# Batch 0's router one unit earlier, its weight transposes ahead of z(61), the last P's lo half shared by GpSimd and VectorE

## The chip, the cores and the metric

One core of a Trainium2 chip runs the whole program. The metric is the device time of one execution in microseconds; the profile of one execution stands beside it. The engines are TensorE (PE, its weight loads PEld), VectorE (DVE), ScalarE (ACT), GpSimd (POOL) and SyncE (SP, which here only issues DMAs). Each engine takes its instructions in program order and waits on semaphores.

## What is computed

An adaLN transformer block in float32 on x of 4 batches x 512 positions x 256 columns:

```
h = layernorm(x) * (1 + ca) + sa
k, q, v = W_K h, W_Q h, W_V h                    # 16 heads of 128
attn = softmax(causal(k.q) / sqrt(128)); z = attn v
x = x + ga * (W_O z)
h = layernorm(x) * (1 + cb) + sb
logits = h @ router_w + router_b - cost          # 8 experts
gate, top = softmax over the two largest of softmax(logits)
out = sum over the two of gate * expert(h @ down_w + down_b)
x = x + gb * ((out + 0.1 shared) @ up_w + up_b + gelu(h) @ core_w + core_b)
```

Every product is made of three TensorE passes on a hi and a lo half of both operands (`mm3`, L680 to L682): hi is the operand rounded to fp32r, lo is the rest, subtracted by VectorE or GpSimd.

## The kernel before, in words

**Order.** One list of events, made by `attention_plan` and `ffn_plan`, is walked by every engine, and each takes from it what is its own, in that order. So the place of an event in the list is its place in up to five queues. Attention runs over 64 units u (4 groups of 4 heads x 4 batches x 4 heads, `unit`), one turn i of the loop per unit, some 10.2 us each. A turn holds the scores S(i+2), q(i+3), `ri` (reciprocal of the sums), k(i+3), `norm` (scaling of P), `wo` (W_O product of an earlier pair), `ty` (VectorE transposes of P in 32x32 blocks, L1076 to L1079), v, `pt`(i+1), z(i) and `tr`(i+2). `fill[i]` is a list of groups of events: the first goes behind S, the next ones behind q, wo, v and z, the rest to the end of the turn. `pre[i]` goes ahead of z(i), `post[i]` to the end.

**P.** `norm` and `ty` leave a transposed P in `gab`; `tr` sends it by four DMAs from SP (L462) to `ptl`, where its blocks come together; `pt` makes its hi half on ScalarE (two casts of 128x640, L650) and its lo half on GpSimd (two subtractions of 128x640, L547, each after its cast). z(u) waits for both (`s_pl`).

**Banks.** The events of `MISC` (q, k, v, z, wo, h, h2, r, wt, dn and others) share three PSUM banks in turn: event m waits until event m-3 is emptied (`me`, counted by VectorE). VectorE empties q, k, v and z by a subtraction (L1049), behind ScalarE's cast (L639).

**Layer norm of the FFN's input** for batch b: `st` steps 0 to 3 (L1004, L1009, L1013) on VectorE, a pow on GpSimd (L490) behind step 3, two pieces `nm` of two 128x256 steps each (L1025), and the transposes `h2` on TensorE (L730). The numbers of `st` and `nm` are 4 + b.

**Router** of batch b: `r` on TensorE (16 small products, L801 and L802) and three VectorE steps (L911 to L914); `rs` 1 to 14 are VectorE steps (L916 to L950), the last of them writes the weights `wg`; four `rp` are pows on GpSimd (L526) that wait for rs 2, and rs 3 (L921) waits for all four; another pow stands between rs 9 and rs 10. `wt` transposes `wg` on TensorE (L859) after rs 14, VectorE copies the result (L1128), and SP stores it to DRAM (L444).

**Weights.** `wh`(n) is the hi cast of piece n on ScalarE (L609) and its lo half on GpSimd (L532, on VectorE for pieces 0, 21 and 22, L987); `ld`(n) is the load by SP, which waits until piece n-2 is done.

**The end of attention before**, as the list has it:

```
S.60 rs1 rs2 q.61 st5.0 ri.60 k.61 norm.60 wo.28.0 st5.1 ty.60 v.30.0 st5.2 pt.59 z.58 st5.3 tr.60 rp0-3
S.61 nm5.0 q.62 nm5.1 ri.61 k.62 norm.61 wo.28.1 ty.61 v.30.1 rs3 pt.60 z.59 rs4 tr.61 h2.1.0
S.62 rs5 q.63 rs6 ri.62 k.63 norm.62 wo.29.0 rs7 ty.62 v.31.0 rs8 pt.61 z.60 rs9 tr.62 h2.1.1
S.63 rs10 ri.63 norm.63 wo.29.1 rs11 ty.63 v.31.1 rs12 pt.62 z.61 rs13 tr.63 rs14 r.1 wt.0 wh.20 ld.22
wo.30.0 st6.0 st6.1 pt.63 z.62 st6.2 st6.3 nm6.0 nm6.1 dn.0 wo.30.1 z.63
```

`r.0` stands right ahead of the first of these lines, at the end of the turn of z(57). dn(0), the first product of the FFN, follows in the list; w1(0), the product behind it, waits for VectorE's lo half of dn(0) (L1189).

Of the kernel before, what the change touches and what calls it, by code (L numbers as in the profile page):

```python
# [5 lines left out]
F32 = mybir.dt.float32  # L6
F32R = mybir.dt.float32r
U32 = mybir.dt.uint32
ALU = mybir.AluOpType
# [4 lines left out]
NU = B * H  # L14
# [30 lines left out]
def attention_plan():  # L45

    pre, post = {}, {}
    fill = {}

    def put(where, i, *events):  # L50
        where.setdefault(i, []).extend(events)
# [3 lines left out]
    for b in (1, 2, 3):  # L55
        i = (0, 2, 5)[b - 1]
# [13 lines left out]
    for b in range(2):  # L70
        fill[54 + 4 * b] = [[("st", B + b, k)] for k in range(4)]
        fill[55 + 4 * b] = [[("nm", B + b, 0)], [("nm", B + b, 1)]]
        put(post, 55 + 4 * b, ("h2", b, 0))
        put(post, 56 + 4 * b, ("h2", b, 1))
        put(post, 57 + 4 * b, ("r", b))
    fill[58] = [[("rs", 0, 1), ("rs", 0, 2)]] + fill[58]
    put(post, 58, *[("rp", 0, c) for c in range(4)])
    fill[59] += [[], [("rs", 0, 3)], [("rs", 0, 4)]]
    fill[60] = [[("rs", 0, k)] for k in range(5, 10)]
    fill[61] = [[("rs", 0, k)] for k in range(10, 15)]  # L80
    put(post, 61, ("wt", 0))
    fill[62] = [[("st", 6, 0), ("st", 6, 1)], [("st", 6, 2)], [("st", 6, 3)], [("nm", 6, 0), ("nm", 6, 1)]]
    put(post, 61, ("wh", 20), ("ld", 22))
    plan = [("b1",), ("mod0",)] + [("st", 0, k) for k in range(4)] + [("silu",), ("wh", 0), ("ld", 2), ("wh", 1), ("ld", 3),
            ("nm", 0, 0), ("nm", 0, 1), ("mod",),
            ("h", 0, 0), ("h", 0, 1), ("wh", 2), ("ld", 4), ("q", 0), ("k", 0), ("v", 0, 0), ("S", 0), ("ri", 0), ("norm", 0), ("ty", 0), ("q", 1), ("k", 1), ("v", 0, 1),
# [6 lines left out]
    for i in range(NU):  # L93
        steps = list(fill.get(i, []))

        def add(*events):
            for ev in events:
                plan.append(ev)
                if steps and ev[0] in ("S", "q", "wo", "z", "v"):
                    plan.extend(steps.pop(0))  # L100

        if i + 2 < NU:
            add(("S", i + 2))
        if i + 3 < NU:
            add(("q", i + 3))
        if i + 2 < NU:
            add(("ri", i + 2))
        if i + 3 < NU:
            add(("k", i + 3))
        if i + 2 < NU:  # L110
            add(("norm", i + 2))
        if i >= 2:
            add(("wo", i // 2 - 1, i % 2))
        if i + 2 < NU:
            add(("ty", i + 2), ("v", i // 2 + 1, i % 2))
        if i + 1 < NU:
            add(("pt", i + 1))
        add(*pre.get(i, []))
        add(("z", i))
        if i + 2 < NU:  # L120
            add(("tr", i + 2))
        plan += [("ld", n) for n in loads.get(i, [])]
        plan += [ev for group in steps for ev in group]
        plan += post.get(i, [])
        if i + 2 == NU:
            plan.append(("dn", 0))
# [85 lines left out]
def build(nc, x, ct, wmod, wat, wfa, wfb, cst, bcol, b2, ub, cb, out, scr, scw):  # L212
# [20 lines left out]
    with ExitStack() as ctx:  # L233
# [3 lines left out]
        def sem(name):  # L237
            return ctx.enter_context(nc.semaphore(name))
# [15 lines left out]
        rs = sb("rs", 16)  # L254
# [12 lines left out]
        with ExitStack() as att:  # L267
# [6 lines left out]
            pth = [sa("pth0", 1280, F32R), sa("pth1", 1280, F32R)]  # L274
            ptl = [sa("ptl0", 1280, F32R), sa("ptl1", 1280, F32R)]
# [21 lines left out]
        mf, mh, me = sem("mf"), sem("mh"), sem("me")  # L297
        s_S, s_M, s_E, s_ty = (sem(n) for n in ("s_S", "s_M", "s_E", "s_ty"))
        s_pt = [sem("s_pt0"), sem("s_pt1")]
        s_ph, s_pl = sem("s_ph"), sem("s_pl")  # L300
        s_v, s_a, s_mh = sem("s_v"), sem("s_a"), sem("s_mh")
        s_ve, s_r0, s_xn = sem("s_ve"), sem("s_r0"), sem("s_xn")
# [42 lines left out]
        def P_blocks(i, j0, n):  # L345

            a = P_OFF[i] + 128 * j0
            return PB[:, a:a + 128 * n].rearrange("p (j s c) -> p j c s", s=32, c=4)

        def Y_blocks(k, n):  # L350

            return Yt.rearrange("p (c k r) -> p k c r", c=4, k=10)[:, k:k + 3 * n - 2:3]
# [124 lines left out]
        def _(pool):  # L477
# [7 lines left out]
            for ev in plan:  # L485
# [26 lines left out]
                if ev[0] == "acc" and ev[2] > 0 and ev not in OWN:  # L512
                    _, t, e = ev
                    i = 8 * t + e - 1
# [26 lines left out]
                                       ALU.add).then_inc(s_y, 1)  # L541
                if ev[0] == "pt":
                    u = ev[1]
                    for c in range(2):
                        s = slice(640 * c, 640 * c + 640)
                        pool.wait_ge(s_ph, 2 * u + c + 1)
                        pool.tensor_tensor(ptl[u % 2][:, s], ptl[u % 2][:, s].bitcast(F32),  # L547
                                           pth[u % 2][:, s].bitcast(F32), ALU.subtract).then_inc(s_pl, 1)
                if ev[0] == "hs":
                    _, t, k = ev  # L550
# [18 lines left out]
                if ev[0] == "up" and ev[1] < B - 1:  # L569
                    _, t, c = ev  # L570
# [107 lines left out]
        def _(pe):  # L678
# [13 lines left out]
            for ev in plan:  # L692
# [29 lines left out]
                elif kind in ("h", "h2"):  # L722
                    _, b, k = ev
# [11 lines left out]
                elif kind in ("q", "k"):  # L735
                    g, b, h = unit(ev[1])
# [10 lines left out]
                elif kind == "v":  # L747
                    _, p, c2 = ev
                    g, b, h = unit(2 * p)
# [6 lines left out]
                elif kind == "S":  # L756
                    u = ev[1]
# [12 lines left out]
                elif kind == "z":  # L770
                    u = ev[1]
                    h = u % 4
                    pe.wait_ge(me, use[("v", u // 2, 1)] + 1)
                    va = (u // 2 % 2) * 1024 + (u % 2) * 128
                    pe.wait_ge(s_pl, 2 * u + 2)
                    for j in range(4):
                        ins = mm3(o[:, 128 * j:512], (vh[:, va + 256 * j:va + 256 * j + 128],
                                                      vl[:, va + 256 * j:va + 256 * j + 128]),
# [13 lines left out]
                elif kind == "r":  # L792
                    b = ev[1]
# [87 lines left out]
        def _(v):  # L881
# [80 lines left out]
            for ev in plan:  # L962
# [28 lines left out]
                elif kind == "st":  # L991

                    _, n, k = ev
                    b = n % B
# [75 lines left out]
                elif kind == "ty":  # L1070
# [6 lines left out]
                    v.wait_ge(s_P3, 4 * u + 4)  # L1077
                    v.transpose(Y_blocks(3, 3), P_blocks(3, 0, 3))
                    v.transpose(Y_blocks(7, 1), P_blocks(3, 3, 1)).then_inc(s_ty, 1)  # L1079
                elif kind == "wo":  # L1080
                    _, p, c2 = ev
                    b = unit(2 * p)[1]
# [198 lines left out]
```

## Time and profile before

| what | value |
|---|---|
| median of 3 runs | 842.51 us (841.69 to 844.74) |
| the profiled execution | 843.71 us, its span 841.9 us |
| TensorE busy | 800.9 us (95%), weight loads 713.0 (85%) |
| VectorE, ScalarE, GpSimd busy | 680.8 (81%), 628.3 (75%), 450.2 us (53%) |
| chain that ended last | TensorE 75%, ScalarE 9%, VectorE 8%, issue 3% |
| mean granted clock | 0.978 of 2.4 GHz |

Times of rows are microseconds from the span's start. A timeline row has the start, the duration, the engine, the line of the kernel, the operation, output <- inputs, and in brackets the idle time just before it with what ended it; `x4` merges four in a row. A granted clock of 1.00 is 2.4 GHz, 0.50 is 1.2 GHz.

### The profile page before, as it was taken

The numbers are of one execution on the slowest core, as the hardware profiler recorded it, in microseconds if no ns is written. First come the engines' busy times: TensorE is split into PE (matmuls) and PEld (weight loads), VectorE is DVE, ScalarE is ACT, GpSimd is POOL, SyncE is SP. The second block draws the span as 40 slices with busy tenths as digits, with TensorE's granted clock in tenths as the row PEclk, the third lists the DMA queues.
The fourth block names the chain that finished last, engine by engine and source line by source line (L and its number), as shares of the span: only waits on it lengthen the run. The fifth ranks groups of instructions, "written<-read, shape, count | busy, mean of one in ns | idle before, by whom it ended". The sixth has DMA issues, their size and how long they took to land.

```text
span 841.9 us, 14484 instructions
## 1 busy us (share of the span) xinstructions
PE 800.9 (95%) x4822; PEld 713.0 (85%) x4822; DVE 680.8 (81%) x1639; ACT 628.3 (75%) x1404; POOL 450.2 (53%) x311
## 2 busy tenths in 40 slices
PE   7778999999999999999999999999999599999997
PEld 6657978999999999999999999998998587788786
DVE  4686998888888888888888788889898787877776
ACT  4566778878887788788887887787877488686874
POOL 3064455664444655544466544575465555566753
PEclk7979999999999999999999999999999799999999
DMA  7233223334222433332234332344222220212131
GB/s 243 72 89 107 63 63 88 88 97 111 63 64 65 112 94 88 91 89 66 64 89 108 100 88 63 78 107 129 65 63 64 69 84 18 76 51 80 47 114 38
DMA packets 47449, 70.54 MB, mean 84 GB/s; under 512 B 5520, under 2 KB 38448, under 8 KB 47248
## 3 DMA queue, kind: packets, MB, share of 16 engines
q1 hardware_dynamic: 46720, 68.28, 30.8%
q0 software_dynamic: 368, 0.81, 0.3%
q8 instruction: 39, 0.64, 0.3%
q10 hardware_dynamic: 288, 0.53, 0.2%
q14 instruction: 34, 0.28, 0.1%
HBM read 25.49 MB, written 2.17 MB: 33 GB/s over the span
## 4 chain that ended last, share of the span: by engine, by line
PE 75%; ACT 9%; DVE 8%; issue 3%; POOL 2%; DMA 2%; SPq 0%; DVEq 0%; POOLq 0%; ACTq 0%
PE M L681 16%; PE M L680 16%; PE M L682 16%; PE S L680 7%; PE S L682 6%; PE S L681 6%; ACT PB L591 3%; PE T L680 2%; PE T L682 2%; PE T L681 2%; ACT PB L626 1%; DVE tmp L1025 1%; DVE S L1060 1%; DVE gab L1076 1%; ACT pth L650 1%
## 5 line engine op out<-in xcount | busy, mean ns | idle before, releaser
L547 POOL TENSOR_TENSOR ptl<-ptl,pth 128x640 fp32r<-128x640 f32 x128 | 198.9, 1576 | 45.0 <-ACT pth L650 45.0
L591 ACT ACTIVATE PB<-S,nb 128x128 f32<-128x128 f32 (+3 forms) x256 | 133.8, 532 | 114.0 <-DVE nb L1060 114.0
L540 POOL TENSOR_TENSOR X<-X,fb 128x512 f32<-128x512 f32 x64 | 83.2, 1301 | 252.1 <-DVE fb L1089 252.1
L626 ACT ACTIVATE PB<-PB,ri 128x256 f32<-128x256 f32 (+3 forms) x256 | 124.4, 579 | 9.4 <-DVE ri L1069 9.3
L1049 DVE TENSOR_TENSOR qk<-M,qk 128x512 fp32r<-128x512 f32 x128 | 88.1, 689 | 53.5 <-ACT qk L639 53.5
L1060 DVE CUSTOM_DVE_ANT_0 S<-S,cc 128x128 f32<-128x128 f32 (+3 forms) x256 | 117.5, 521 | 2.3 <-PE S L682 2.3
L1076 DVE STREAM_TRANSPOSE gab<-PB 128x256 f32<-128x256 f32 (+2 forms) x192 | 109.5, 623 | 1.1 <-ACT PB L626 0.6
L680 PE MATMUL M<-hh,W 128*128 128x512 f32 x264 | 103.8, 393 | 0.2 <-DVE hl L1035 0.2
L681 PE MATMUL M<-hl,W 128*128 128x512 f32 x264 | 103.3, 391 | 0.0
L682 PE MATMUL M<-hh,W 128*128 128x512 f32 x264 | 103.1, 391 | 0.0
L680 PE MATMUL S<-qk 128*128 128x128 f32 (+3 forms) x256 | 88.0, 344 | 4.6 <-DVE qk L1049 4.6
L650 ACT CAST pth<-ptl 128x640 fp32r<-128x640 f32 x128 | 87.7, 743 | 3.5 <-DMA ptl<-gab 3.5
L673 ACT ACTIVATE Gr<-S,bc 128x512 fp32r<-128x512 f32 x84 | 58.5, 696 | 34.3 <-PE S L682 34.3
L682 PE MATMUL S<-qk 128*128 128x128 f32 (+3 forms) x256 | 83.5, 326 | 0.0
L681 PE MATMUL S<-qk 128*128 128x128 f32 (+3 forms) x256 | 83.4, 326 | 0.0
L681 PE MATMUL M<-ptl,vh 128*128 128x512 f32 (+3 forms) x256 | 83.4, 326 | 0.0
L682 PE MATMUL M<-pth,vl 128*128 128x512 f32 (+3 forms) x256 | 83.0, 324 | 0.0
L1203 DVE TENSOR_TENSOR Gr<-S,Gr 128x512 fp32r<-128x512 f32 x84 | 57.4, 687 | 31.2 <-ACT S L674 29.1
L680 PE MATMUL M<-pth,vh 128*128 128x512 f32 (+3 forms) x256 | 81.0, 316 | 1.6 <-DVE qk L1049 1.1
L639 ACT CAST qk<-M 128x512 fp32r<-128x512 f32 x128 | 75.9, 594 | 6.7 <-PE M L682 6.4
L680 PE MATMUL M<-W,hh 128*128 128x256 f32 x256 | 73.6, 287 | 6.5 <-DVE qk L1049 6.1
L681 PE MATMUL M<-W,hh 128*128 128x256 f32 x256 | 72.7, 284 | 0.0
(181 smaller groups left out, 2310.5 us busy)
## 6 DMA issues: line engine op xcount, KB each, us to landing
ptl<-gab SPq DMA_DIRECT2D x256, 160.0 KB, 3.1
stage<-in_wat SPq DMA_DIRECT2D x16, 512.0 KB, 4.9
gab<-scw SPq DMA_DIRECT2D x16, 256.0 KB, 3.3
tmp<-scw SPq DMA_DIRECT2D x16, 256.0 KB, 3.5
X<-in_x SPq DMA_DIRECT2D x4, 512.0 KB, 5.3
stage<-in_wfa SPq DMA_DIRECT2D x3, 512.0 KB, 4.4
out<-X SPq DMA_DIRECT2D x3, 512.0 KB, 2.6
X<-in_wmod SPq DMA_DIRECT2D x1, 1024.0 KB, 6.5
```

Of the source, the lines that this page charges most:

```text
L540: pool.tensor_tensor(X[:, a:a + 512], X[:, a:a + 512], fb[:, c2 * 512:c2 * 512 + 512], ALU.add).then_inc(s_y, 1)
L547: pool.tensor_tensor(ptl[u % 2][:, s], ptl[u % 2][:, s].bitcast(F32), pth[u % 2][:, s].bitcast(F32), ALU.subtract).then_inc(s_pl, 1)
L591: ins = act.activation(PB[:, P_OFF[i]:P_OFF[i] + w], PS[bk][:, a:a + w], ACT.Exp, bias=nb[:, i:i + 1], scale=-1.0, accum_out=sm[:, i:i + 1])
L626: act.activation(p, p, ACT.Copy, scale=ri[:, i:i + 1]).then_inc(s_P3, 1)
L639: act.copy(dst, src).then_inc(mh, 1)
L650: act.copy(pth[u % 2][:, s], ptl[u % 2][:, s].bitcast(F32)).then_inc(s_ph, 1)
L680: pe.matmul(o, lhs[0], rhs[0], start=start, stop=False, **kw)
L681: pe.matmul(o, lhs[0], rhs[1], start=False, stop=False, **kw)
L682: return pe.matmul(o, lhs[1], rhs[0], start=False, stop=stop, **kw)
L1049: v.tensor_tensor(lo, src, hi.bitcast(F32), ALU.subtract).then_inc(me, 1)
L1060: ins = v.tensor_tensor_reduce(PS[bk][:, a:a + w], PS[bk][:, a:a + w], mask[:, 512 - w:512], -INV, BIG, ALU.add, ALU.min, nb[:, i:i + 1])
L1076: v.transpose(Y_blocks(i, i + 1), P_blocks(i, 0, i + 1))
```

## The change

Batch 0's r(0) goes ahead of z(57), inside the turn at whose end it stood, and its steps rs and rp move with it: rs 1 and 2 behind z(57), the pows at the end of that turn, rs 3 behind S(60), rs 14 behind wo(29,1). wt(0) goes ahead of z(61). pt(63) goes behind z(62); its second lo half is done by VectorE, which waits for both casts, and z(63) waits for it with a semaphore of its own (`s_pv`). wh(20) and ld(22) go to the end of the turn of z(62). The same stretch of the list then reads:

```
... v.29.1 pt.58 r.0 z.57 rs1 rs2 tr.59 rp0-3
S.60 rs3 st5.0 q.61 rs4 st5.1 ri.60 k.61 norm.60 wo.28.0 st5.2 ty.60 v.30.0 st5.3 pt.59 z.58 tr.60
S.61 nm5.0 q.62 nm5.1 ri.61 k.62 norm.61 wo.28.1 rs5 ty.61 v.30.1 rs6 pt.60 z.59 rs7 tr.61 h2.1.0
S.62 rs8 rs9 q.63 ri.62 k.63 norm.62 wo.29.0 rs10 ty.62 v.31.0 rs11 pt.61 z.60 rs12 tr.62 h2.1.1
S.63 rs13 ri.63 norm.63 wo.29.1 rs14 ty.63 v.31.1 pt.62 wt.0 z.61 tr.63 r.1
wo.30.0 st6.0 st6.1 z.62 st6.2 pt.63 st6.3 nm6.0 nm6.1 wh.20 ld.22 dn.0 wo.30.1 z.63
```

```diff
--- before.py
+++ after.py
@@ -72,15 +72,17 @@
         fill[55 + 4 * b] = [[("nm", B + b, 0)], [("nm", B + b, 1)]]
         put(post, 55 + 4 * b, ("h2", b, 0))
         put(post, 56 + 4 * b, ("h2", b, 1))
-        put(post, 57 + 4 * b, ("r", b))
-    fill[58] = [[("rs", 0, 1), ("rs", 0, 2)]] + fill[58]
-    put(post, 58, *[("rp", 0, c) for c in range(4)])
-    fill[59] += [[], [("rs", 0, 3)], [("rs", 0, 4)]]
-    fill[60] = [[("rs", 0, k)] for k in range(5, 10)]
-    fill[61] = [[("rs", 0, k)] for k in range(10, 15)]
-    put(post, 61, ("wt", 0))
+    put(pre, 57, ("r", 0))
+    put(post, 61, ("r", 1))
+    fill[57] = [[], [], [], [], [("rs", 0, 1), ("rs", 0, 2)]]
+    put(post, 57, *[("rp", 0, c) for c in range(4)])
+    fill[58] = [[("rs", 0, 3)] + fill[58][0], [("rs", 0, 4)] + fill[58][1]] + fill[58][2:]
+    fill[59] += [[("rs", 0, k)] for k in range(5, 8)]
+    fill[60] = [[("rs", 0, 8), ("rs", 0, 9)], [], [("rs", 0, 10)], [("rs", 0, 11)], [("rs", 0, 12)]]
+    fill[61] = [[("rs", 0, 13)], [("rs", 0, 14)]]
+    put(pre, 61, ("wt", 0))
     fill[62] = [[("st", 6, 0), ("st", 6, 1)], [("st", 6, 2)], [("st", 6, 3)], [("nm", 6, 0), ("nm", 6, 1)]]
-    put(post, 61, ("wh", 20), ("ld", 22))
+    put(post, 62, ("wh", 20), ("ld", 22))
     plan = [("b1",), ("mod0",)] + [("st", 0, k) for k in range(4)] + [("silu",), ("wh", 0), ("ld", 2), ("wh", 1), ("ld", 3),
             ("nm", 0, 0), ("nm", 0, 1), ("mod",),
             ("h", 0, 0), ("h", 0, 1), ("wh", 2), ("ld", 4), ("q", 0), ("k", 0), ("v", 0, 0), ("S", 0), ("ri", 0), ("norm", 0), ("ty", 0), ("q", 1), ("k", 1), ("v", 0, 1),
@@ -113,10 +115,12 @@
             add(("wo", i // 2 - 1, i % 2))
         if i + 2 < NU:
             add(("ty", i + 2), ("v", i // 2 + 1, i % 2))
-        if i + 1 < NU:
+        if i + 2 < NU:
             add(("pt", i + 1))
         add(*pre.get(i, []))
         add(("z", i))
+        if i + 2 == NU:
+            add(("pt", i + 1))
         if i + 2 < NU:
             add(("tr", i + 2))
         plan += [("ld", n) for n in loads.get(i, [])]
@@ -297,6 +301,7 @@
         mf, mh, me = sem("mf"), sem("mh"), sem("me")
         s_S, s_M, s_E, s_ty = (sem(n) for n in ("s_S", "s_M", "s_E", "s_ty"))
         s_pt = [sem("s_pt0"), sem("s_pt1")]
+        s_pv = sem("s_pv")
         s_ph, s_pl = sem("s_ph"), sem("s_pl")
         s_v, s_a, s_mh = sem("s_v"), sem("s_a"), sem("s_mh")
         s_ve, s_r0, s_xn = sem("s_ve"), sem("s_r0"), sem("s_xn")
@@ -541,7 +546,7 @@
                                        ALU.add).then_inc(s_y, 1)
                 if ev[0] == "pt":
                     u = ev[1]
-                    for c in range(2):
+                    for c in range(2 if u + 1 < NU else 1):
                         s = slice(640 * c, 640 * c + 640)
                         pool.wait_ge(s_ph, 2 * u + c + 1)
                         pool.tensor_tensor(ptl[u % 2][:, s], ptl[u % 2][:, s].bitcast(F32),
@@ -772,7 +777,9 @@
                     h = u % 4
                     pe.wait_ge(me, use[("v", u // 2, 1)] + 1)
                     va = (u // 2 % 2) * 1024 + (u % 2) * 128
-                    pe.wait_ge(s_pl, 2 * u + 2)
+                    pe.wait_ge(s_pl, 2 * u + 2 - (u + 1 == NU))
+                    if u + 1 == NU:
+                        pe.wait_ge(s_pv, 1)
                     for j in range(4):
                         ins = mm3(o[:, 128 * j:512], (vh[:, va + 256 * j:va + 256 * j + 128],
                                                       vl[:, va + 256 * j:va + 256 * j + 128]),
@@ -1077,6 +1084,11 @@
                     v.wait_ge(s_P3, 4 * u + 4)
                     v.transpose(Y_blocks(3, 3), P_blocks(3, 0, 3))
                     v.transpose(Y_blocks(7, 1), P_blocks(3, 3, 1)).then_inc(s_ty, 1)
+                elif ev == ("pt", NU - 1):
+                    s = slice(640, 1280)
+                    v.wait_ge(s_ph, 2 * NU)
+                    v.tensor_tensor(ptl[1][:, s], ptl[1][:, s].bitcast(F32), pth[1][:, s].bitcast(F32),
+                                    ALU.subtract).then_inc(s_pv, 1)
                 elif kind == "wo":
                     _, p, c2 = ev
                     b = unit(2 * p)[1]
```

## Rows read from the trace of the kernel before

**Rows 1.** Waits of TensorE, whole span: line, waited for, us, times, longest.
```profile
PE M L859 <- DVE wg L950: 9.2, 2, 7.0
...
PE T L680 <- DVE stage L1147: 0.7, 1, 0.7
```

**Rows 2.** Timeline of TensorE: start us, us, engine, line, output<-inputs [idle before].
```profile
33.30 0.48 PE L680 MATMUL S<-qk 128*128 128x128 f32 x1 [2.96 <-DVE qk L1049]
...
620.20 0.28 PE L680 MATMUL M<-W,hh 128*128 128x256 f32 x1
...
640.43 0.39 PE L680 MATMUL M<-W,hh 128*128 128x256 f32 x1 [0.80 <-DVE qk L1049]
...
644.40 0.31 PE L680 MATMUL S<-qk 128*128 128x128 f32 x1
...
649.45 0.28 PE L682 MATMUL M<-W,hl 128*128 128x256 f32 x1
...
661.48 1.01 PE L859 MATMUL M<-cc,wg 128*8 128x128 f32 x4 [7.05 <-DVE wg L950]
...
670.23 0.47 PE L680 MATMUL M<-pth,vh 128*128 128x512 f32 x1 [0.54 <-POOL ptl L547]
...
673.21 0.50 PE L680 MATMUL S<-ur,W 128*128 128x512 f32 x1 [0.86 <-DVE ur L1189]
```

**Rows 3.** Timeline of VectorE around the reduction of S(60).
```profile
615.10 0.57 DVE L914 TENSOR_TENSOR rt<-rt,cc 128x32 f32<-128x32 f32 x1
...
617.35 0.17 DVE L916 TENSOR_REDUCE rt<-rt 128x4 f32<-128x32 f32 x1
...
618.25 0.69 DVE L1049 TENSOR_TENSOR qk<-M,qk 128x512 fp32r<-128x512 f32 x1 [0.50 <-ACT qk L639]
618.85 0.74 DVE L1004 BATCH_NORM_STATS2 mv<-X 128x6 f32<-128x256 f32 x2
```

**Rows 4.** Timeline of GpSimd, 590 to 675 us.
```profile
612.54 3.08 POOL L547 TENSOR_TENSOR ptl<-ptl,pth 128x640 fp32r<-128x640 f32 x2 [0.29 <-ACT pth L650]
...
627.33 6.45 POOL L526 TENSOR_TENSOR rt<-ebase,rt 128x8 f32<-128x8 f32 x4
...
657.94 2.34 POOL L532 TENSOR_TENSOR W<-stage,W 128x1024 fp32r<-128x1024 f32 x1
...
670.04 1.02 POOL L490 TENSOR_TENSOR rs<-rs 128x4 f32<-128x4 f32 x1
```

**Rows 5.** Timelines of GpSimd, VectorE and TensorE, 584 to 589 us.
```profile
584.64 3.16 POOL L547 TENSOR_TENSOR ptl<-ptl,pth 128x640 fp32r<-128x640 f32 x2
...
585.84 2.10 DVE L1025 TENSOR_SCALAR tmp<-X,mv,rs 128x256 f32<-128x256 f32 x2
...
588.60 0.39 PE L680 MATMUL M<-W,hh 128*128 128x256 f32 x1 [0.90 <-DVE qk L1049]
```

**Rows 6.** Timeline of VectorE, the router's step 12 of batch 0.
```profile
657.96 2.35 DVE L946 TENSOR_TENSOR rt<-rt 128x4 f32<-128x4 f32 x1
```

**Rows 7.** Timelines of VectorE, SP's queue and ScalarE, end of attention.
```profile
652.47 1.71 DVE L1076 STREAM_TRANSPOSE gab<-PB 128x256 f32<-128x256 f32 x3
...
655.14 0.66 DVE L1049 TENSOR_TENSOR vl<-M,vh 128x512 fp32r<-128x512 f32 x1
...
655.26 2.61 SPq L462 DMA_DIRECT2D ptl<-gab  x4
...
660.43 1.35 ACT L650 CAST pth<-ptl 128x640 fp32r<-128x640 f32 x2 [3.50 <-DMA ptl<-gab]
...
671.17 1.38 DVE L1025 TENSOR_SCALAR tmp<-X,mv,rs 128x256 f32<-128x256 f32 x4 [2.52 <-POOL rs L490]
```

**Rows 8.** Windows: stretch, length, busy PE, PEld, DVE, ACT, POOL, PEclk, DMA, GB/s.
```profile
33.20:33.40 0.20, 0.10 (x1) 0.10 (x1) 0.20 (x2) 0.00 (x0) 0.00 (x0) 0.50 0.10 19
...
664.60:664.70 0.10, 0.10 (x3) 0.10 (x2) 0.00 (x0) 0.00 (x0) 0.00 (x0) 0.69 0.26 102
```

**Rows 9.** Timeline of VectorE: a lo half whose two inputs lie in SBUF.
```profile
676.45 1.23 DVE L987 TENSOR_TENSOR W<-stage,W 128x1024 fp32r<-128x1024 f32 x1 [0.21 <-ACT W L609]
```

## The prediction

> **What bounds the kernel now.** I read the page first: TensorE is busy for 95% of 841.9 us, and its tenths are 9 in nearly every slice but one, near 650 to 670 us, where attention hands over to the FFN. The table of TensorE's waits names the hole: of 9.2 us spent waiting for the router weights wg, one wait has 7.0 us [rows 1]. TensorE's timeline places it: unit 61's values end at 649.7 us, z(61) and batch 1's router follow, then the weight transposes wt(0) start only at 661.48, after 7.05 us of nothing, and the first FFN product, w1(0), at 673.21 [rows 2]. Everything before is a chain of units of some 10.2 us in which TensorE is nearly full, so a delay there is carried to w1(0), and from w1(0) on TensorE is nearly full again. The sum below therefore follows one number: how far w1(0) moves. All times are on the clock of this profile.
>
> VectorE and GpSimd were read next. In this trace a VectorE step whose inputs lie in SBUF stands still while GpSimd runs a long SBUF piece: a 128x4 product takes 2.35 us, from 657.96 to the end of GpSimd's W piece of 2.34 us [rows 4, 6], and two layer-norm pieces take 2.10 us beside GpSimd's P halves [rows 5] where four take 1.38 us alone [rows 7]. L914 takes 0.57 us and ends with GpSimd's piece [rows 3, 4].
>
> **Part 1: the router a unit earlier.** r(0) now stands ahead of z(57), rs 1 and 2 behind z(57), the four pows behind them on GpSimd, and rs 3 right behind S(60)'s reduction on VectorE. TensorE does the same work in another order and starts S(60) at the same time. On VectorE L914 again ends when GpSimd's P piece does (612.54 + 3.08 = 615.62), now ahead of z(57)'s lo half (0.6) and of rs 1 and 2 (0.2 each): 616.7. The four pows take 6.45 us [rows 4], so they end at 623.2. VectorE has only S(60)'s reduction (the 1.7 us between L914 and L916 in [rows 3]) to do meanwhile, is through at 618.4, and then waits in rs 3 for some **4.8 us**. Queued behind it are the first statistics (0.74, 0.66 apart), q(61)'s lo half, ri(60), k(61), the W_O product and unit 60's transposes. v(30,0) on TensorE needs the bank that q(61) frees: 623.2 + 0.2 + 0.7 + 0.7 = 624.8 in place of 620.20 [rows 2, 3]. A **new hole of 4.7 us**, since TensorE had reached that point at 620.2. Before, a whole unit lay between the pows and rs 3, so this wait cost nothing. I see no bound below 4 us: the pows would have to be shorter than their row.
>
> Second, with rs 3 and 4 merged in front, batch 1's last statistics step, and the pow that GpSimd does for it, come ahead of pt(59), no longer behind it. That is the order in which batch 0's stand now: there GpSimd's halves begin at 584.64, the two layer-norm pieces beside them take 2.10 us, and TensorE waits 0.90 us at 588.60 [rows 5]. With VectorE already late I take **1.2 us** (0.9 to 1.5). Third, the wait of 0.80 us at 640.43 [rows 2] falls in a unit whose GpSimd queue had been held by the pows; they are gone, and I give back half: **-0.4** (0 to -0.8). S(63) thus starts 4.7 + 1.2 - 0.4 = **5.5 us later**, at 649.9 in place of 644.40.
>
> **Part 2: wt(0) ahead of z(61).** rs 14 is done just before unit 63's transposes start, 8.07 us after S(63) (652.47 - 644.40) [rows 2, 7]: 658.0. TensorE ends the values at 649.7 + 5.5 = 655.2, so wt(0) still waits, now 2.9 us in place of 7.05, with z(61) and r(1) queued behind it. They then run beside VectorE's transposes, and wo(30,0), z(62), dn(0) and wo(30,1) follow without a long hole, to about 669.5.
>
> SP's queue pays: the store of the weights is now ahead of tr(63), the four DMAs of the last P. It waits for VectorE's copy, which stands behind the transposes and the values (652.47 to 655.80, 3.33 us) and takes 0.6 (a 512-column step, as the values' 0.66): 661.9. Its issue costs about one of the four in 2.61 us, 0.6. From the first P issue to ScalarE's start is 660.43 - 655.26 = 5.2 us [rows 7]: 667.7. Before, tr(63) went out as soon as the transposes ended, so this is 1.8 us that TensorE's gain has to carry.
>
> **Part 3: the last lo half shared.** ScalarE's first half takes 0.7 (668.4), GpSimd's half 1.55 (half of 3.08): 669.95. VectorE's half has no row; the nearest, 128x1024 in 1.23 us [rows 9], makes 0.75, and it reads two SBUF tiles, so it waits for GpSimd's half: 670.7. Bounds: 669.95 (both at once) to 671.5 (no faster than GpSimd). The two halves in a row cost 0.8 us less than GpSimd's 3.1.
>
> The Trainium skill, "SBUF — State Buffer", SBUF: two separate sides, says that VectorE and GpSimd share one port pair, an exclusive lock held for a whole instruction by whichever starts first. By it the halves don't overlap and w1(0) comes at the time below; if they could, it would come 0.75 us earlier. [rows 6] agree with the lock.
>
> **Part 4: the W piece behind it.** wh(20) leaves the old hole, where it cost nothing but VectorE's 2.35 us, and stands on GpSimd directly behind the layer-norm pow of batch 2. st 3 (0.2) gives 670.9, the pow (1.02) 671.9. At that moment the W piece, long ready, starts, and VectorE's four layer-norm pieces (dn(0)'s lo half behind them) are released by a semaphore, which costs VectorE 0.11 us after a pow (671.17 against 670.04 + 1.02) [rows 4, 7]. So GpSimd is first: 671.9 + 2.34 = 674.25, then the pieces (one ends with the lock, three more 1.0) 675.3, dn(0)'s lo half 0.66, w1(0) at **676.0** against 673.21 [rows 2]: **+2.8 us**. ScalarE's share of wh(20) (about 1 us) and its table load lie under this.
>
> **The clock.** The granted clock is at half (0.50) when a hole of 2.96 us ends at 33.30, and after the 7.05 us one; it came back about 3.2 us after work resumed, at 664.6 [rows 2, 8]. Half speed for that long costs 1.6 us. Before wt(0) that loss falls away with most of its hole, already inside w1(0)'s time. In the 4.7 us hole it falls too, but VectorE reaches S(61) only at about 631, nearly 3 us after TensorE could start it, and hides 1.6. z(63) takes 2.1 us (670.23 to 673.21 less the 0.86 of waiting), from 670.7 to 672.8, and then TensorE waits 3.2 us for w1(0): the clock falls, and of 1.6 us the 0.7 us wait on L1147 [rows 1] and what ScalarE and VectorE set there anyway take 0.9. **+0.7.**
>
> **Sum.** +2.8 + 0.7 = +3.5 us. The profiled run took 843.71 us (span 841.9 and 1.8 around it), the median of the runs is 842.51, 1.2 less; I add to the median: **846.0 us**.
>
> **The rivals.** *Half speed is carried* (slower). The place is the 4.7 us hole and the start of the FFN; if VectorE is ahead of S(61) rather than behind (decided at TensorE starting it later than about 630.5), the first fall costs its 1.5, and at w1(0) the whole 1.6 counts: 2.8 + 1.5 + 1.6 = +5.9, 848.4. For it: two holes that long; against: VectorE's queue behind rs 3.
>
> *The layer norm gets in first.* If a VectorE piece starts ahead of the W piece, GpSimd waits instead: pieces 672.0 to 673.4, w1(0) 674.1, hole 1.3 us and no fall: +0.9, 843.4. Against it: 0.11 us of semaphore. The Trainium skill, "SBUF — State Buffer", SBUF: two separate sides, gives the ports to whoever starts first; this is the case in which that favours VectorE.
>
> *The early wait is hidden* (faster). If the pows were done when VectorE gets to rs 3, S(63) stays at 644.40, w1(0) comes 2.7 us earlier than before, the fall costs 0.7: -2.0, 840.5. Against it: 6.45 us of pows and 1.7 us of cover.
>
> **How the numbers follow.** Forecast 0.52, carried half speed 0.25, layer norm first 0.13, early wait hidden 0.07, something else 0.03. A measurement here tells about 0.5% (4.2 us: 838.3 to 846.7) from no change. Of the forecast's own spread (844.5 to 847.2, from the bounds above) about 0.09 lies over 846.7: slower 0.25 + 0.09 = 0.34, faster 0.04 (part of the hidden case and the rest), same 0.62. The range runs from below the layer-norm case, 842.0, to above the carried case, 849.0.
>
> **What would show it.** Right: an idle VectorE of some 4.8 us ahead of L921, released by GpSimd's pow, and TensorE waiting over 4 us for q's L1049 near 620 to 625; L859 waiting about 3 us; the P issues behind the weight store; a layer-norm piece of over 2 us at 672 to 674 that ends with the W piece; half clock at w1(0). Wrong: VectorE passing L921 without a wait, S(63) less than 4 us late, or w1(0) before 673.

## The result, and the profile after

The changed kernel takes **849.6 us** in the median of nine runs (845.9 to 851.9); the kernel before takes 843.27 us in nine runs of the same series (841.7 to 844.7). The ratio is 1.0069, with a 95% interval of 1.0052 to 1.0087, so the change costs some 5.8 us (4.4 to 7.3). The forecast was 846.0 us with a range up to 849.0: the sign was right, the size was not, and the time lies 0.6 us outside the range.

The profiled execution of the changed kernel takes 848.26 us, 4.55 us more than that of before. Its page, span, busy times and the granted clock by slice:

```profile
span 846.4 us, 14485 instructions
...
PE 805.6 (95%) x4822; PEld 716.6 (85%) x4822; DVE 680.6 (80%) x1640; ACT 627.8 (74%) x1404; POOL 448.6 (53%) x310
...
PEclk7989999999999999999999999999989899999999
```

TensorE has the same number of instructions and 4.7 us more busy time (800.9 before), so part of what was lost is not waiting but the same work at a lower clock. The timeline of TensorE shows the waits that answer to [rows 2], and the one ahead of wt(1), which follows with its counterpart in the trace of before:

```profile
623.18 0.58 PE L685 MATMUL M<-W,hh 128*128 128x256 f32 x1 [4.37 <-DVE qk L1056]
...
648.35 0.31 PE L685 MATMUL S<-qk 128*128 128x128 f32 x1
...
656.14 0.60 PE L866 MATMUL M<-cc,wg 128*8 128x128 f32 x4 [2.79 <-DVE wg L957]
...
669.96 0.47 PE L685 MATMUL M<-pth,vh 128*128 128x512 f32 x1 [0.87 <-DVE ptl L1090]
...
675.08 0.52 PE L685 MATMUL S<-ur,W 128*128 128x512 f32 x1 [3.01 <-DVE ur L1201]
...
719.83 1.01 PE L866 MATMUL M<-cc,wg 128*8 128x128 f32 x4 [2.17 <-DVE wg L957]
```

and before:

```profile
716.87 0.60 PE L859 MATMUL M<-cc,wg 128*8 128x128 f32 x4 [2.16 <-DVE wg L950]
```

The 7.05 us hole of before has become 2.79 us. Two others have come: 4.37 us at v(30,0), where there was none, and 3.01 us ahead of w1(0), where there were 0.86. VectorE's and GpSimd's timelines name their causes:

```profile
615.13 6.45 POOL L531 TENSOR_TENSOR rt<-ebase,rt 128x8 f32<-128x8 f32 x4 [1.05 <-DVE rt L925]
...
621.68 0.19 DVE L928 TENSOR_REDUCE rt<-rt 128x4 f32<-128x32 f32 x1 [4.80 <-POOL rt L531]
...
667.55 1.58 POOL L552 TENSOR_TENSOR ptl<-ptl,pth 128x640 fp32r<-128x640 f32 x1 [1.91 <-ACT pth L655]
668.13 1.68 DVE L1090 TENSOR_TENSOR ptl<-ptl,pth 128x640 fp32r<-128x640 f32 x1 [0.28 <-ACT pth L655]
...
670.96 2.35 POOL L537 TENSOR_TENSOR W<-stage,W 128x1024 fp32r<-128x1024 f32 x1
...
671.10 3.33 DVE L1032 TENSOR_SCALAR tmp<-X,mv,rs 128x256 f32<-128x256 f32 x4 [1.21 <-POOL rs L495]
```

The first 600 us, which the change doesn't touch, differ between any two executions (S(60) starts at 614.07 us in the profile of before, at 612.53 in this one). So executions are set side by side from the start of S(60). Each number is a start in us behind it; the columns are the last scores, the weight transposes of batch 0, ScalarE's cast of z(62), w1(0), the last transposes of batch 2, the weight transposes of batch 1, the first product of the weights behind them (L873 in the changed kernel), and the end; the last column adds up the granted clock's time at half over the 128 us behind S(60), as the sum over windows of 1 us of (1 - PEclk) / 0.5.

| execution | S(63) | wt(0) | z(62) cast | w1(0) | h2(2,1) | wt(1) | L873 | end | at half |
|---|---|---|---|---|---|---|---|---|---|
| before | 30.33 | 47.41 | 52.79 | 59.14 | 69.77 | 102.80 | 107.53 | 227.83 | 10.2 |
| after | 35.82 | 43.61 | 53.73 | 62.55 | 74.27 | 107.30 | 113.58 | 233.87 | 17.1 |
| e1_rs3_late | 30.75 | 38.53 | 48.69 | 57.50 | 69.22 | 102.25 | 106.97 | 227.33 | 6.8 |
| e2_wh20_back | 35.83 | 43.62 | 56.01 | 62.87 | 73.50 | 106.53 | 112.72 | 233.07 | 17.1 |
| e3_gpsimd_both | 36.36 | 44.01 | 53.17 | 62.61 | 73.23 | 106.29 | 111.03 | 231.32 | 10.3 |
| e4_filled | 35.49 | 43.18 | 53.42 | 62.25 | 72.89 | 105.84 | 110.58 | 230.89 | 3.4 |
| e5_rs3_wh20 | 30.76 | 38.54 | 47.60 | 54.46 | 65.08 | 98.11 | 102.84 | 223.11 | 3.4 |
| e8_fill_early | 35.49 | 43.29 | 55.70 | 64.53 | 76.22 | 109.27 | 115.56 | 235.90 | 17.1 |
| e9_fill_wt1 | 35.52 | 43.31 | 55.65 | 64.49 | 76.18 | 109.17 | 113.92 | 234.31 | 17.1 |
| e10_e5_wt0_back | 30.74 | 41.72 | 47.39 | 54.25 | 64.87 | 97.91 | 102.64 | 222.95 | 3.4 |
| e11_e5_fill_wt1 | 30.75 | 38.54 | 50.90 | 57.76 | 68.37 | 101.32 | 106.06 | 226.35 | 10.2 |
| e12_e5_gpsimd_both | 30.73 | 38.52 | 50.89 | 58.36 | 68.97 | 102.01 | 106.75 | 227.10 | 10.2 |

In the rows of before and after, the delay is 5.5 us at S(63), 3.4 at w1(0), 4.5 at h2(2,1) and at wt(1), 6.0 at L873 and at the end. So the forecast's +2.8 at w1(0) was 0.6 short, and behind w1(0), where it had +0.7, another 2.6 us come. A profiled execution need not be the median one: that of e3 is 4.9 us below the median of its runs, that of e1 1.8 below, that of e12 2.8 above. So the traces are compared stage by stage, and whole times by their medians.

### The profile page after: what moved, and what is told of

Read it like the earlier page. It is cut to its first block, busy times and chain, and to the rows that moved or that the text cites. A ratio compares the mean times of both kernels' runs of the same rounds, so it can differ in the third digit from the quotient of the medians.

```text
span 846.4 us, 14485 instructions
## 1 busy us (share of the span) xinstructions
PE 805.6 (95%) x4822; PEld 716.6 (85%) x4822; DVE 680.6 (80%) x1640; ACT 627.8 (74%) x1404; POOL 448.6 (53%) x310
## 3 DMA queue, kind: packets, MB, share of 16 engines
HBM read 25.49 MB, written 2.17 MB: 33 GB/s over the span
## 4 chain that ended last, share of the span: by engine, by line
PE 71%; ACT 11%; DVE 10%; issue 4%; DMA 2%; POOL 1%; SPq 1%; DVEq 0%; POOLq 0%
PE M L685 15%; PE M L686 15%; PE M L687 15%; PE S L685 6%; PE S L687 6%; PE S L686 6%; ACT PB L596 3%; PE T L685 2%; PE T L687 2%; PE T L686 2%; DVE gab L1083 2%; DVE S L1067 2%; ACT PB L631 1%; DVE tmp L1032 1%; ACT pth L655 1%
```

## The experiments

Edits are given against the changed kernel, or against the version named. Ratios are to the kernel before, run on the same chip.

**rs 3 late.** rs 3 goes behind z(58), rs 4 behind S(61).

```diff
-    fill[58] = [[("rs", 0, 3)] + fill[58][0], [("rs", 0, 4)] + fill[58][1]] + fill[58][2:]
+    fill[58] += [[("rs", 0, 3)]]
+    fill[59][0] = [("rs", 0, 4)] + fill[59][0]
```

> The changed kernel with one edit: the router's steps 3 and 4 of batch 0 stand behind z(58) and S(61) again, so that the four pows have a unit to themselves; statistics steps and all else as in the change. Theory A (VectorE's in-order wait for the pows is the main loss): no wait ahead of the reduction of step 3, no TensorE hole over 4 us at v(30,0); S(63) 4 to 5 us earlier than in the changed kernel, time 4 to 6 us below it, near 844. Theory B (the early wait is hidden by VectorE's slack later, the loss lies at the end of attention): the hole goes but w1(0) comes less than 1 us earlier, time as the changed kernel, 849. Theory C (the lost time is half clock, whatever opens the holes): 1 to 2 us below the changed kernel.

Measured: 843.11 us, ratio 0.999 (0.9971 to 1.0009), against 1.0069 for the whole change: 6.7 us less with rs 3 and 4 later, and the intervals lie apart. In TensorE's timeline v(30,0) starts without a wait (618.27, 6.1 us behind S(60), as before). A wait of 0.77 us is left a unit later, at v(30,1), and the hole ahead of w1(0) stays:

```profile
618.27 0.28 PE L686 MATMUL M<-W,hh 128*128 128x256 f32 x1
...
628.60 0.38 PE L686 MATMUL M<-W,hh 128*128 128x256 f32 x1 [0.77 <-DVE qk L1057]
...
669.67 0.75 PE L686 MATMUL S<-ur,W 128*128 128x512 f32 x1 [3.01 <-DVE ur L1202]
```

S(63) is back at 30.75, 5.1 us earlier than in the changed kernel and 0.4 later than before. At wt(1) the two profiles part by another 1.6 us, since there the clock fell in that of the change and didn't in this one; whether the rest of the 6.7 us of the medians is that, no run shows.

The 0.77 us are the prediction's second term by itself. On VectorE the first two layer-norm pieces of batch 1 stand beside GpSimd's P halves and take 1.99 us:

```profile
625.96 1.99 DVE L1033 TENSOR_SCALAR tmp<-X,mv,rs 128x256 f32<-128x256 f32 x2
```

S(62) is 1.0 us later than before by it (20.22 against 19.25), and 0.5 of that are given back by S(63).

**The W piece back.** wh(20) and ld(22) return to the end of the turn of z(61).

```diff
-    put(post, 62, ("wh", 20), ("ld", 22))
+    put(post, 61, ("wh", 20), ("ld", 22))
```

> The changed kernel with one edit: the W piece wh(20) and its load stand at the end of the turn of z(61) again, ahead of pt(63). Theory A (the lock by GpSimd's W piece delays batch 2's layer norm by its length): the four layer-norm pieces take about 1.4 us in place of 3.3, w1(0) 2 us earlier against dn(0), the hole ahead of it about 1 us, too short for the clock to fall, so 2 to 3 us below the changed kernel. Theory B (VectorE would be held by something else anyway, ScalarE's table load and gelu of dn(0)): under 0.7 us.

Measured: 849.64 us, ratio 1.0054 (1.0036 to 1.0073), which the times alone can't tell from the change. In the trace VectorE isn't held up by the W piece any more (the prediction's lock): the four layer-norm pieces take 1.38 us in place of 3.33, and the hole ahead of w1(0) is 1.06 us.

```profile
674.57 1.38 DVE L1032 TENSOR_SCALAR tmp<-X,mv,rs 128x256 f32<-128x256 f32 x4 [1.21 <-POOL rs L495]
...
676.60 0.50 PE L685 MATMUL S<-ur,W 128*128 128x512 f32 x1 [1.06 <-DVE ur L1201]
```

From ScalarE's cast of z(62) to w1(0) it takes 6.86 us in place of 8.82, so the W piece costs 1.96 us. But w1(0) comes no earlier, since z(62) itself is 2.3 us later: in this execution the granted clock stands at half for 10.2 us around wt(0), z(61) and r(1), in the profiled execution of the changed kernel for 3.4. That made the clock the next question.

**Both halves on GpSimd.** pt(63) stays behind z(62).

```diff
-                    for c in range(2 if u + 1 < NU else 1):
+                    for c in range(2):
...
-                    pe.wait_ge(s_pl, 2 * u + 2 - (u + 1 == NU))
-                    if u + 1 == NU:
-                        pe.wait_ge(s_pv, 1)
+                    pe.wait_ge(s_pl, 2 * u + 2)
...
-                elif ev == ("pt", NU - 1):
-                    s = slice(640, 1280)
-                    v.wait_ge(s_ph, 2 * NU)
-                    v.tensor_tensor(ptl[1][:, s], ptl[1][:, s].bitcast(F32), pth[1][:, s].bitcast(F32),
-                                    ALU.subtract).then_inc(s_pv, 1)
```

> The changed kernel with one edit: both lo halves of the last P on GpSimd, pt(63) still behind z(62). Theory A (the halves cannot overlap, VectorE's is only shorter): z(63) 0.8 to 0.9 us later and w1(0) 0.7 us later than in the changed kernel; time up by 0.7, within noise. Theory B (the halves overlap in part): up by 1.5. Theory C (VectorE's half costs as much as it gains, since the layer norm stands behind it): no change.

Measured: 850.71 us, ratio 1.0066 (1.0045 to 1.0088), no difference from the change. In the trace z(63) waits 1.67 us for GpSimd in place of 0.87 for VectorE, and from the cast of z(62) to w1(0) it takes 9.44 us in place of 8.82: the sharing is worth 0.6 us there, too little for these times.

```profile
670.35 0.48 PE L685 MATMUL M<-pth,vh 128*128 128x512 f32 x1 [1.67 <-POOL ptl L552]
```

**The holes filled.** 60, 30, 36 and 24 unused 128x128 products go into TensorE's holes ahead of v(30,0), wt(0), w1(0) and wt(1). They add work whose result nothing reads.

```diff
+            HOLE = {('v', 30, 0): 60, ('wt', 0): 30, ('w1', 0): 36, ('wt', 1): 24}
             for ev in plan:
                 kind = ev[0]
+                if ev in HOLE and kind != "wt":
+                    warm(HOLE[ev])
...
+                if ev in HOLE and kind == "wt":
+                    for _ in range(HOLE[ev]):
+                        pe.matmul(o[:, 0:128], Dz[:], Dz[:], start=True, stop=True)
```

> The changed kernel with unused 128x128 bf16 products on zeros put into TensorE's four holes: 60 ahead of v(30,0), 30 ahead of wt(0), 36 ahead of w1(0), 24 ahead of wt(1), each less than its hole at full clock. The waits stay. Theory A (half clock after the holes is 2 to 3 us of the loss): granted clock 1.00 after each hole, w2 and the rest of the FFN's start 1 us earlier, no fall at wt(1), time 2 to 3 us below the changed kernel and its spread between runs smaller. Theory B (half clock is hidden by waits on VectorE): same time as the changed kernel.

Measured: 846.43 us, ratio 1.0021 (1.0001 to 1.004). The order of the work is that of the change, and yet 0.48% come back, 4.0 us, with intervals that lie apart. So half speed is worth about 4 us of the changed kernel's time. That isn't yet the clock's part in the change, since the kernel before has half speed too (its holes are filled further down). Between the two profiles the filling gains 3.0 us: 0.3 up to S(63), 1.1 behind w1(0) and 1.5 at wt(1). Around r(1) it gains nothing, the clock falls there all the same (17.9 us from S(63) to the cast of z(62) in both). Where the early fall is gone, S(61) comes 2.0 us earlier (14.05 against 16.04 behind S(60)) but S(63) only 0.3 (35.49 against 35.82): the early fall is all but hidden, as forecast.

**Both orders back.** rs 3 late and the W piece back together, the two edits above.

> The changed kernel with two edits: the router's steps 3 and 4 late, as in e1_rs3_late, and the W piece wh(20) with its load ahead of pt(63) again, as in e2_wh20_back. What is left of the change: the router a unit earlier, wt(0) ahead of z(61), the split lo half. Theory A (queue waits add up): the hole ahead of w1(0) is 1 us in place of 3 and w1(0) 2 us earlier than in e1_rs3_late, time 1.5 to 3 us below e1_rs3_late, 840 to 841.5, below the kernel before. Theory B (as e2_wh20_back alone, which moved the time little): as e1_rs3_late, 843.

Measured: 839.27 us, ratio 0.9945 (0.9928 to 0.9961): 0.55% faster than before. From e1 to this one, the W piece alone makes 0.45%, 3.8 us, with intervals apart: 1.96 us of waiting for the W piece, and the clock's fall behind the 3.01 us hole (1.1 us from w1(0) to h2(2,1) in the profiles), which isn't there any more (at half for 6.8 us in e1's profile, 3.4 in this one).

**The same with holes filled**, 30, 12 and 24 unused products ahead of wt(0), w1(0) and wt(1).

> As e5_rs3_wh20, with unused 128x128 bf16 products on zeros in the three holes left: 30 ahead of wt(0), 12 ahead of w1(0), 24 ahead of wt(1). Theory A (half clock costs even where the holes are under 3 us): 2 to 3 us below e5_rs3_wh20, near 838, faster than the kernel before by over 0.5%. Theory B (the clock falls only after the longer holes): as e5_rs3_wh20.

Measured: 840.07 us, ratio 0.9947 (0.9927 to 0.9967): the filling gives nothing that these times could tell. The windows of its trace (stretch, length, busy PE, PEld, DVE, ACT, POOL, PEclk, DMA, GB/s) show one reason: the fall comes all the same, on r(1)'s small products of 16 columns.

```profile
656.00:657.00 1.00, 1.00 (x5) 1.00 (x6) 0.15 (x1) 0.00 (x0) 1.00 (x2) 0.50 0.42 55
```

**The kernel before with its holes filled**, 80 and 24 unused products ahead of wt(0) and wt(1).

> The kernel before with unused 128x128 bf16 products on zeros in its two holes: 80 ahead of wt(0) (4.5 of 7.05 us), 24 ahead of wt(1). All waits stay. Theory A (half clock behind the 7.05 us hole costs what the rows show): wo(30,0) runs at full clock, 1.3 us less there and up to 1.5 at wt(1) in the executions in which it falls, so 1.5 to 2.5 us below the kernel before, 841 to 842. Theory B (what is late there is VectorE's, not the clock's): no change. Against e4_filled it shows what the change costs when both run at full clock: A, 2 to 4 us.

Measured: 842.1 us, ratio 0.998 (0.9966 to 0.9994), 1.7 us less: in the old order, too, half speed had a price. With e4 this gives the clock's part in the change: with holes filled the change costs 1.0021 / 0.998, 0.41% or 3.5 us, in place of 5.8, so some 2.3 us of it are the clock's. This is an estimate: the three intervals leave about 2.5 us either way, and neither filling takes all of the half speed away (3.4 us of it are left in each of the two profiles). The medians alone don't tell 2.3 from the forecast's 0.7; the traces show where the time goes.

**The changed kernel with only the early hole filled**, 60 unused products ahead of v(30,0).

> The changed kernel with 60 unused bf16 products in its new hole ahead of v(30,0) alone; the other holes stay empty. All four filled took 4 us off. Theory A (the fall in the early hole is hidden behind VectorE, as predicted): under 0.7 us below the changed kernel, 849. Theory B (it is carried through to S(63)): 1.3 to 1.6 us, 848. Theory C (each fall also shifts when the next holes find the clock falling): any amount with a wide spread of single times.

Measured: 848.28 us, ratio 1.0034 (1.0016 to 1.0053), 2.9 us below the change by the ratios, whose intervals just touch. The profiled execution, the slowest of its six, shows S(63) at 35.49, 0.3 us earlier than in the change, so in it the early hole's own gain is small; and it has the clock at half for 17.1 us, as the changed kernel has. I can't say from these runs what the filling did in the others.

**The changed kernel with only the hole ahead of wt(1) filled**, 24 unused products.

> The changed kernel with 24 unused 128x128 products ahead of wt(1), in the 2.17 us hole of the FFN's start, and nothing else. In the profile of the changed kernel the clock falls behind this hole and the stretch from wt(1) to the down products takes 6.28 us instead of 4.73 of before. Theory 'the fall at wt(1) belongs to the change's time': filled, that stretch takes 4.7 to 4.8 us and the median comes down by 1.5 us, to 848.1. Rival 'it came in that one execution only, or the next stage hides it': the median stays within 0.5 us of 849.6.

Measured: 847.5 us, ratio 1.0039 (1.002 to 1.0058), 2.5 us below the change, with intervals that overlap at their ends. The fall at wt(1) is gone: from wt(1) to L873 it takes 4.75 us in place of 6.28. It fits the price of 1.5 us, but doesn't pin it. The execution has the long stretch around r(1), with w1(0) at 64.49, and runs of this kernel spread from 844.2 to 851.8.

**Against e5_rs3_wh20: wt(0) back behind r(1).**

```diff
-    put(post, 61, ("r", 1))
+    put(post, 61, ("r", 1), ("wt", 0))
...
-    put(pre, 61, ("wt", 0))
```

> The version with rs 3 late and the W piece back in its old place, and in addition wt(0) back behind r(1), as before the change. The prediction held the store of the weights ahead of tr(63) to cost the last P 1.8 us. Theory 'the store holds up the last P': wt(0) now comes without a hole behind r(1) (z(61) and r(1) fill the 2.78 us), the last P goes out 1.5 to 2 us earlier and w1(0) comes up to 1.8 us earlier than 54.46 us behind S(60): 837.5 to 838.5 us. Rival 'VectorE's queue sets the last P anyway': w1(0) within 0.5 us of the 54.46, 839.3 us.

Measured: 839.32 us, ratio 0.9932 (0.9909 to 0.9955), not to be told from 0.9945. SP's queue shows the effect that the forecast priced: the four DMAs of the last P now stand ahead of the store of the weights and go out 41.13 us behind S(60), 1.64 earlier than in e5 (42.77).

```profile
656.48 2.57 SPq L467 DMA_DIRECT2D ptl<-gab  x4
659.89 0.36 SPq L449 DMA_DIRECT2D scw<-rows  x1
```

But w1(0) moves by 0.2 us only (54.25 against 54.46): the last P's cast stands behind z(62)'s cast on ScalarE, and that one waits for TensorE. The store holds the DMAs up and costs nothing here. wt(0) ahead of z(61) gains nothing either, so e5's 0.55% come from what is left: the router a unit earlier, the last P's casts behind z(62), and the halves shared. No run takes the first two apart.

**e5_rs3_wh20 with only the hole ahead of wt(1) filled**, 24 unused products.

> The version with rs 3 late and the W piece back, with the 24 unused products ahead of wt(1) alone. Its profile without them shows no fall there (wt(1) to the down products 4.73 us behind a hole of 2.17). Theory 'whether the clock falls behind a hole of 2.2 us is a matter of the execution': without a fall to take away the median stays at 839.3 (within 0.5). Rival 'most executions have the fall and the profiled one was the exception': 1.5 us less, 837.8.

Measured: 841.04 us, ratio 0.9949 (0.9929 to 0.9969): no different from e5. That fits executions without a fall to take away, though 1.5 us lie within what the two intervals leave open. The profile shows something else. Up to wt(1) this kernel and e5 do the same work in the same order, and in both TensorE reaches wt(0) at 38.54; yet ScalarE's cast of z(62) comes at 47.60 in the one and at 50.90 in the other. ScalarE's row and a window of each, e5 first:

```profile
661.39 0.59 ACT L645 CAST zt<-M 128x512 fp32r<-128x512 f32 x1 [3.61 <-PE M L688]
```

```profile
659.00:660.00 1.00, 1.00 (x7) 0.87 (x7) 1.00 (x1) 0.00 (x0) 1.00 (x1) 1.00 0.87 213
```

and e11:

```profile
665.15 0.59 ACT L645 CAST zt<-M 128x512 fp32r<-128x512 f32 x1 [7.36 <-PE M L688]
```

```profile
659.00:660.00 1.00, 1.00 (x5) 1.00 (x6) 0.32 (x2) 0.00 (x0) 1.00 (x1) 0.50 0.97 169
```

TensorE is busy through both windows; the clock is 1.00 in one and 0.50 in the other. In e5 it fell 0.3 us before wt(0) and was back after 3.4 us, in e11 it fell 1.2 us behind wt(0)'s start, during z(61), and stayed at half for 10.2 us. Those 3.3 us go on to w1(0) and to the end, and the profiled times of the two differ by 3.7 us (838.74 and 842.42).

**e5_rs3_wh20 with both halves on GpSimd**, the edit of e3.

> The version with rs 3 late and the W piece back, with both lo halves of the last P on GpSimd again (still behind z(62)). The prediction put the sharing at 0.8 us gained, with the halves one behind the other under the lock. If so, z(63) and w1(0) come 0.7 to 0.9 us later than in the version with the halves shared, and the median is 840.0; if ScalarE's casts or the clock hide it, 839.3.

Measured: 840.14 us, ratio 0.9944 (0.9923 to 0.9966), no different from e5. From the cast of z(62) to w1(0) it takes 7.47 us in place of 6.86: the sharing is worth 0.61 us, as in e3.

## Why the prediction was right or wrong

**The early hole: right.** VectorE waits 4.80 us in rs 3 for the pows (forecast 4.8), TensorE 4.37 us at v(30,0) (forecast 4.7, though the sum's own 624.8 and 620.20 make 4.6), and S(63) is 5.49 us late (5.5); e1 takes 5.1 of it back. The three terms can be read where the clock is out of the way, in e4: S(61) is 4.6 us late (4.7), S(62) 5.7, so 1.1 for the second term (1.2), and S(63) 5.2, so 0.6 are given back (0.4). e1 has the same last two, 1.0 and 0.5. Half speed in this hole makes S(61) 2.0 us later and S(63) 0.3: it is hidden, nearly as forecast. So the rival of a hidden wait falls, and so do the 1.5 us that the rival of a carried half speed lost here, although its 848.4 us came nearest.

**wt(0): right in its hole, wrong in what follows.** The hole is 2.79 us (forecast 2.9; its 658.0 and 655.2 make 2.8). The store ahead of the last P costs its DMAs 1.64 us (forecast 1.8), as e10 shows, but it isn't on the path, which goes through z(62): on ScalarE the last P's casts follow the cast of z(62), and that one waits 6.79 us for TensorE.

```profile
666.26 0.58 ACT L644 CAST zt<-M 128x512 fp32r<-128x512 f32 x1 [6.79 <-PE M L687]
666.74 1.36 ACT L655 CAST pth<-ptl 128x640 fp32r<-128x640 f32 x2
```

The casts were forecast for 667.7 on the clock of before, where 666.74 is 668.28 (1.54 us added): 0.6 us late, the 0.6 that w1(0) has over the forecast. That the two lie so close is in part luck. In this profile the clock stands at half during the W_O product ahead of z(62), which costs 1.1 us up to the cast; without it (as in e3) w1(0) would be about +2.3 us and not +3.4, by an estimate from these rows, and the forecast's +2.8 came between the two from a wait that isn't on the path.

**The halves: right.** VectorE's half begins beside GpSimd's, at 668.13, and ends 0.68 us after it (669.81 against 669.13; forecast 0.75); the sharing gains 0.6 us (forecast 0.8).

**The W piece: right.** GpSimd is first by 0.14 us (670.96 and 671.10), the layer norm of batch 2 takes 3.33 us, and the hole is 3.01 us (forecast 3.2). The rival in which the layer norm gets in first falls; its price, 1.9 us, is what e2 measured (1.96). The Trainium skill, "SBUF — State Buffer", SBUF: two separate sides, has the lock held for a whole instruction by whichever starts first; the 3.33 us beside the piece and 1.38 without it agree.

**The clock: this is the step that failed.** The sum had +0.7 us for it. In the profile of the change half speed costs 1.1 us ahead of w1(0) (0.6 of them beyond the forecast), 1.1 behind it and 1.55 at wt(1); by the medians of the filled kernels, less what it costs before, it is some 2.3 (4.0 of e4 less 1.7 of e7). Three steps were wrong or missing:

- "Before wt(0) that loss falls away with most of its hole, already inside w1(0)'s time." The hole is shorter, but the fall stays. The trace of before could have warned of it: there the clock goes to half at 654.4, right behind r(1)'s last product and as the hole begins, not after a long wait (two windows of that trace, columns as in e6's: PE is the first busy share, PEclk stands third from the end):

```profile
653.07:654.07 1.00, 1.00 (x12) 1.00 (x11) 1.00 (x3) 1.00 (x3) 0.71 (x1) 1.00 0.00 0
654.07:655.07 1.00, 0.35 (x4) 0.26 (x3) 1.00 (x3) 1.00 (x3) 0.12 (x1) 0.68 0.00 0
```

Of the 10.2 us at half 7.05 lay inside the hole, where no work was slowed down. In the new order TensorE has z(61), r(1) and the W_O product to do, and the cast of z(62), on which w1(0) hangs, waits for their end. The clock falls within 0.3 us of wt(0)'s start (e3, e5, e10), during z(61) (e2, e8, e9, e11, e12), or on r(1) or right behind it (the change, e1, e4, e6). From S(63) to that cast it takes 16.8 us in e5 and e3, where the clock is back at 1.00 before the W_O product, 17.9 in the profile of the change, where it is at half during it, and 20.2 in e2 and e11 with the long stretch: up to 3.3 us by the execution, 1.1 in the profiled one, of which 0.6 show against the forecast.
- At w1(0) the fall cost 1.1 us (3.4 us late there, 4.5 at h2(2,1)), where 0.7 was forecast. From w1(0) to h2(2,1) it takes 11.7 us in the change and in e1, where the clock falls, and 10.6 in e3, where it doesn't behind a hole of 2.81 us:

```profile
675.29 0.50 PE L685 MATMUL S<-ur,W 128*128 128x512 f32 x1 [2.81 <-DVE ur L1194]
```

- wt(1) has no place in the sum: its hole is the same, 2.17 us against 2.16. But the clock falls behind it in this execution and did not in that of before; the four transposes take 1.01 us in place of 0.60, and the stretch up to L873 6.28 in place of 4.73, another **1.55 us**. This was seen in three profiles (the change, e2 and e8) and not in those of before, e1, e3, e5, e10 and e12. No run shows how often it comes in the kernel before, so whether the change brings it or the execution does stays open.

A window of each of the three stretches at half in the profile of the change (columns as above):

```profile
662.00:663.00 1.00, 1.00 (x7) 1.00 (x6) 0.00 (x0) 0.00 (x0) 0.00 (x0) 0.50 0.94 173
...
677.00:678.00 1.00, 1.00 (x5) 0.81 (x5) 0.17 (x1) 1.00 (x3) 0.00 (x0) 0.50 0.08 16
...
721.00:722.00 1.00, 1.00 (x4) 0.74 (x3) 1.00 (x1) 0.00 (x0) 1.00 (x2) 0.50 0.00 0
```

In these windows TensorE is fully busy: a stretch at half is no wait and stands in no table of waits, so a sum made of waits doesn't see it.

**The sum.** From S(60) to the end the profiled execution takes 6.04 us more than that of before, where the forecast had 3.5. It is 5.49 us late at S(63), wins 4.55 back up to the cast of z(62), as the old hole is shorter, and loses 2.47 from there to w1(0): +3.41. Behind w1(0) come 1.1 us of the fall there and 1.55 at wt(1). Over the forecast that is 0.6 us at w1(0), 0.4 more of the fall there (1.1 against 0.7) and 1.55 at wt(1), together 2.55, and in each of these places TensorE works at half speed. The median of nine runs, 849.6, is 1.3 us above this execution. Single times go with the mean granted clock, from 845.88 us at 0.978 to three of 850.40 to 851.93 at 0.972; the long stretch around r(1) would make such times, but no trace of these executions shows it. And 0.8 us are the base: the median of before was 842.51 us over three runs and is 843.27 over nine.

**What stays open.** How the 4.0 us of the medians are split between the stretches, and how much of them the change brings: the ratios of e4, e8 and e9 overlap, and whether a stretch is short or long changes from one execution to the next by more than one filling gains. What decides whether the clock falls behind a hole of 2.2 us, these runs don't show.

## What to carry to other kernels

A step moved earlier in a list that every engine walks must be costed on the engine that waits for it: rs 3 cost 5.1 us at S(63), and 6.7 by the medians, because VectorE stood behind four pows of GpSimd with TensorE's next bank queued behind it; with rs 3 most of a turn later in the same list VectorE doesn't wait for the pows at all. Moved like that, and with the W piece left where it doesn't hold up VectorE's layer norm, the change is worth 0.55% (e5_rs3_wh20), while as made it loses 0.69%. When a hole is shortened and not closed, look where in the old trace the clock falls, and price the half speed by the work that will run there: in the old hole 7.05 of 10.2 us at half cost nothing, in the new order they fall on work that others wait for.

## What the runs showed of the hardware

- Behind a hole of TensorE of the same length the granted clock goes to 0.50 in one execution and not in another. Ahead of wt(1), behind 2.16 to 2.17 us, it fell in three profiles (the change, e2, e8) and didn't in six (before, e1, e3, e5, e10, e12); ahead of w1(0) it fell behind 3.01 us in the change and in e1 and didn't behind 2.81 in e3.
- The length at half varies as well, with the same instructions: 3.4 us in e5, 10.2 in e11, a difference of 3.3 us in the time at which z(62) was ready.
- Filling a hole with unused products didn't always keep the clock up: in e6 it fell on r(1)'s products of 16 columns, at 655.4 us, and stood at half for 6.8 us.
- A VectorE step of 128x4 is held up like a large one: st 3 takes 1.25 us beside GpSimd's P halves in VectorE's timeline of e12, and 0.16 in that of the change.

```profile
666.52 1.25 DVE L1019 TENSOR_SCALAR rs<-mv 128x4 f32<-128x4 f32 x1
```

```profile
669.73 0.16 DVE L1020 TENSOR_SCALAR rs<-mv 128x4 f32<-128x4 f32 x1
```
